# Scale factors of the first four heads from a quarter of the key and query weights, and the tail's squares in slots 10 to 15

## What is computed

```python
x = x + attn_a(layernorm(x))     # q = xn @ Wq[h] + bq, k = xn @ Wk[h] + bk, v = xn @ Wv[h] + bv
                                 # softmax(causal(q @ k.T / 8)) @ v per head, then @ Wo + bo
x = x + ffn(layernorm(x))        # relu(xn @ w1 + b1) @ w2 + b2
x = x + attn_b(layernorm(x))
x = x + ffn(layernorm(x))
```

## Time and profile before

| | us |
|---|---|
| median of 3 runs | 563.05 (561.37 to 563.49) |
| the profiled execution, first to last instruction | 561.3 |
| prologue, to the first instruction of slot 0 | 35.3 |
| one slot in the middle | 11.7 |

### The profile page before, as it was taken

How to read it: one execution, slowest core, us unless ns; L and a number is a source line. 1 busy time by engine, 2 the same in 40 slices (tenths; PEclk the granted TensorE clock), 3 DMA queues, 4 the chain that set the end, 5 groups by cost and what they waited for, 6 DMA issues and landing times.

```text
span 561.3 us, 17932 instructions
## 1 busy us (share of the span) xinstructions
PE 526.3 (94%) x6864; PEld 371.1 (66%) x6864; DVE 446.3 (80%) x1382; ACT 469.0 (84%) x925; POOL 453.8 (81%) x447
## 2 busy tenths in 40 slices
PE   4888999999999999999999999998989998798897
PEld 3654666666666666766667666675679695656576
DVE  5878888888888888888888888887785575788943
ACT  3888998999988999989999899998973978573995
POOL 5678989888888888888888888888983977654885
PEclk9979999999999999999999999999999999998999
DMA  9442343332433324333243332435147100000002
GB/s 227 109 113 57 72 110 86 96 96 68 114 87 97 95 64 118 87 95 96 60 122 80 102 97 58 124 78 198 40 151 272 68 3 2 1 1 2 1 21 57
DMA packets 35461, 48.03 MB, mean 86 GB/s; under 512 B 10777, under 2 KB 16817, under 8 KB 35377
## 3 DMA queue, kind: packets, MB, share of 16 engines
q1 hardware_dynamic: 33264, 46.35, 30.2%
q10 hardware_dynamic: 2112, 0.54, 0.4%
HBM read 12.27 MB, written 9.44 MB: 39 GB/s over the span
## 4 chain that ended last, share of the span: by engine, by line
PE 75%; DVE 8%; issue 6%; ACT 5%; POOL 5%; DMA 1%; DVEq 0%; POOLq 0%; ACTq 0%
PE psum L562 11%; PE psum L620 10%; PE psum L621 10%; PE psum L516 7%; PE psum L518 6%; PE psum L517 6%; PE psum L600 6%; PE psum L602 6%; PE psum L601 6%; PE psum L623 2%; POOL h_lo L2146 1%; PE psum L781 1%; POOL rstd L2024 1%; ACT xn L1164 1%; DVE st_lo L1515 1%
## 5 line engine op out<-in xcount | busy, mean ns | idle before, releaser
L2079 POOL TENSOR_TENSOR p_hl<-p,p_hl 128x512 f16<-128x512 f32 x288 | 328.5, 1165 | 48.4 <-ACT p_hl L1264 44.6
L1532 DVE CUSTOM_DVE_ANT_0 max_junk<-psum,mask_s 128x1024 bf16<-128x1024 f32 (+7 forms) x256 | 190.4, 753 | 32.7 <-issue 32.6
L1263 ACT ACTIVATE p<-psum 128x512 f32<-128x512 f32 x288 | 175.9, 611 | 13.8 <-PE psum L623 12.2
L1264 ACT ACTIVATE p_hl<-psum 128x512 f16<-128x512 f32 x288 | 177.2, 615 | 0.0
L620 PE MATMUL psum<-q_hl,k_hh 128*128 128x512 f16 (+3 forms) x384 | 125.6, 327 | 0.5 <-ACT p_hl L1264 0.4
L600 PE MATMUL psum<-v_all,p_hl 128*128 128x65 f16 x1152 | 124.8, 193 | 1.1 <-POOL p_hl L2079 1.0
L601 PE MATMUL psum<-v_all,p_hl 128*128 128x64 f16 x1152 | 124.9, 192 | 0.0
L602 PE MATMUL psum<-v_all,p_hl 128*128 128x65 f16 x1152 | 124.4, 194 | 0.0
L621 PE MATMUL psum<-q_hm,k_l 128*128 128x512 f16 (+3 forms) x384 | 122.3, 327 | 0.0
L600 PEld LDWEIGHTS psum<-v_all,p_hl 128*128 128x128 f16 x1152 | 107.1, 98 | 16.1 <-POOL p_hl L2079 1.2
L601 PEld LDWEIGHTS psum<-v_all,p_hl 128*128 128x128 f16 x1152 | 106.2, 97 | 4.8
(11 more groups left out here) (206 smaller groups left out, 1109.1 us busy)
## 6 DMA issues: line engine op xcount, KB each, us to landing
k_hh<-st_hi SPq DMA_DIRECT2D x64, 128.0 KB, 2.3
o_scratch<-o_sb SPq DMA_DIRECT2D x16, 512.0 KB, 2.6
o_in<-o_scratch SPq DMA_DIRECT2D x8, 1024.0 KB, 8.6
q_hl<-st_hi SPq DMA_DIRECT2D x32, 128.0 KB, 2.4
q_hl<-st_lo SPq DMA_DIRECT2D x32, 128.0 KB, 2.4
k_l<-st_lo SPq DMA_DIRECT2D x32, 128.0 KB, 2.3
q_hm<-st_hi SPq DMA_DIRECT2D x32, 128.0 KB, 2.4
x_sb<-in_L_attn_a_x SPq DMA_DIRECT2D x4, 256.0 KB, 3.9
```

The lines of the kernel that those rows point to most:

```text
L1263: nc.scalar.activation(p32[:, ring_at(u, r), :], src, ACT.Exp, scale=SCALE_A).then_inc(exp_done, 1)
L1264: nc.scalar.activation(p_hl[:, u % 2, 0, BANK * r:BANK * (r + 1)], src, ACT.Exp, scale=SCALE_A).then_inc(phi_done, 1)
L1532: nc.vector.tensor_tensor_reduce(out=max_junk[:, n % 2, 0:cols], in0=max_banks(v, j, 0, cols), in1=mask_s[:, S - cols:S], scale=1.0, scala ...
L2079: nc.gpsimd.tensor_tensor(p_hl[:, u % 2, 1, cols], p32[:, ring_at(u, r), :], p_hl[:, u % 2, 0, cols], ALU.subtract)\
```

## The change

- **Loads.** Wk and Wq are each loaded in two DMAs: heads 0 to 3 (a quarter) first, then the rest. The load of Wo comes after x chunks 2 and 3. The small loads (`bo`, `W_qk`, `W_v`, slope, `b1`, `b2`) are issued after the copies of the first pair.
- **Gains.** Heads 0 to 3 get key and query gains of their own from the first quarter and its biases. The other twelve heads get theirs later, in the middle of the maximum tiles of head 0 (`norm_kq(1)`, `gain_kq(1)`, `scale_bias(1)`). The roots are taken by integer steps on VectorE: the difference of two bit patterns, a quarter of it, the exponent bits. The powers on GpSimd and their operands `fourths` are gone.
- **Orders.** The pieces go in the order 0, 2, 1, 3. The square of Wv comes after their eviction. ScalarE now makes the scaled high half and the scaled copy of the rest of Wv. `first_stats(2)` stands before the low half of Wv, the first two maximum tiles stand between the value units, and the two `rest_scale` that are left stand between later maximum tiles. The counts and places of `idle_products` differ.
- **GpSimd and VectorE.** The memset of `k_l1` moves to the start of GpSimd's list and that of `q_hm` to the start of VectorE's. The memset of the rows of `k_l1` (8 partitions x 2048) now follows the second `chunk_rstd` and three selects.
- **Tail.** The six squares stand in slots 10 to 15, one each, ahead of that slot's last exponentials. Their sum, the transpose, `tail_norm` and `tail_gain` stand in slot 16, without GpSimd's power, and `tail_scales` in slots 17 to 19.

The core of the diff (declarations left out):

```diff
             load_x(0)
             load_x(1)
-            sp.dma_start(w_raw[:, 0, :].rearrange(...), Wk.rearrange("h e d -> e h d")).then_inc(wk_in, 16)
-            sp.dma_start(w_raw[:, 2, :].rearrange(...), Wv.rearrange("h e d -> e h d")).then_inc(wv_in, 16)
-            sp.dma_start(wo_raw[:, :, :], Wo.rearrange("(k p) e -> p k e", p=P)).then_inc(wo_in, 16)
-            sp.dma_start(bo_sb[:, :], bo.unsqueeze(1)).then_inc(bo_in, 16)
+            load_heads(0, Wk, 0, GH, wk_in[0])
+            load_heads(0, Wk, GH, H, wk_in[1])
+            load_heads(2, Wv, 0, H, wv_in)
             load_x(2)
             load_x(3)
+            sp.dma_start(wo_raw[:, :, :], Wo.rearrange("(k p) e -> p k e", p=P)).then_inc(wo_in, 16)
...
+            idle_products(14, 5)
+            pe.wait_ge(ones_ready, 1)
+            norm_sums(0, MAXB + 1)
             turn_chunk(0)
-            idle_products(8, 5)
+            idle_products(10, 5)
             turn_chunk(1)
-            idle_products(8, 5)
-            pe.wait_ge(sq_done, 4)
-            pe.wait_ge(ones_ready, 1)
-            nc.tensor.matmul(bank(MAXB + 1)[:, 0:4], ones[:, :], sums[:, 0:4], start=True, stop=True).then_inc(fro_full, 1)
-            idle_products(32, 5)
-            pe.wait_ge(first_lo, 2)
-            pe.wait_ge(xt_lo_done, 2)
-            for n in range(2):
+            idle_products(4, 5)
+            for n in FIRST_ORDER:
+                pe.wait_ge(first_lo, n // 2 + 1)
+                pe.wait_ge(xt_lo_done, n % 2 + 1)
                 piece(n, FIRST_BANKS[n])
...
+            values(0, V_BANKS[0])
+            max_tile(0, 0)
+            values(1, V_BANKS[1])
+            max_tile(0, 1)
+            values(2, V_BANKS[2])
+            values(3, V_BANKS[3])
+            norm_sums(1, V_BANKS[0])
+            max_tile(0, 2)
+            piece(4, V_BANKS[1])
+            max_tile(0, 3)
+            piece(5, V_BANKS[2])
+            max_tile(0, 4)
+            idle_products(8, 4)
...
+                nc.vector.tensor_tensor(apart, norms[:, k].bitcast(I32), norms[:, q].bitcast(I32), ALU.subtract).then_inc(root_done, 1)
+                nc.vector.tensor_scalar(quarter, apart, 0.25, QUARTER_ONE, ALU.mult, ALU.add).then_inc(root_done, 1)
+                nc.vector.tensor_scalar(gains[:, q].bitcast(I32), quarter, POW2, None, ALU.bitwise_and).then_inc(gain_made, 1)
...
             chunk_norm(0)
+            norm_kq(0, MAXB + 1)
+            gain_kq(0)
             chunk_norm(1)
-            norm_kq()
             chunk_low(0)
-            gain_kq()
-            chunk_low(1)
...
             norm_v()
             gain_v()
+            first_stats(2)
             first_low(2)
+            first_stats(3)
             dve.wait_ge(tri_ready, 2)
+            take_max(0, 0)
+            take_max(0, 1)
+            norm_kq(1, V_BANKS[0])
+            gain_kq(1)
+            scale_bias(1)
+            rest_scale(0)
+            take_max(0, 2)
+            rest_scale(1)
+            take_max(0, 3)
...
                 exponentials(u, 7)
+                if u in SQUARE_AT:
+                    tail_square(SQUARE_AT[u])
                 exponentials(u, 8)
```

More of the change, by code:

```diff
@@ L624, in scores, with idle_products @@
                 last.then_inc(st_full, 1)
+            def idle_products(n, dst):
+                for _ in range(n):
+                    nc.tensor.matmul(bank(dst)[:, 0:P], ident_b[:, :], ident_b[:, :], start=True, stop=True)
             def pe_slot(u):
@@ L701, in pe_slot @@
                     turn_chunk(3)
+                if u == SUMS_AT:
+                    pe.wait_ge(v_lo_done, units_after(u))
+                    pe.wait_ge(tail_sq, 6)
+                    nc.tensor.matmul(bank(MISC)[:, 3 * P:3 * P + 6], ones[:, :], tail_sums[:, :], start=True, stop=True).then_inc(prep_full, 1)
+                    nc.tensor.transpose(bank(MISC)[:, P:2 * P], wv2_raw[:, :], ident[:, :]).then_inc(prep_full, 1)
                 scores(u, 7)
@@ L707, in pe_slot @@
                 scores(u, 8)
-            def idle_products(n, dst):
-                for _ in range(n):
-                    nc.tensor.matmul(bank(dst)[:, 0:P], ident_b[:, :], ident_b[:, :], start=True, stop=True)
             pe.wait_ge(bias_in, 48)
@@ L732, in _ @@
-            for n in range(2, 4):
-                piece(n, FIRST_BANKS[n])
-            idle_products(12, 5)
+            idle_products(4, 5)
+            for n in FIRST_ORDER:
+                pe.wait_ge(first_lo, n // 2 + 1)
+                pe.wait_ge(xt_lo_done, n % 2 + 1)
+                piece(n, FIRST_BANKS[n])
+            idle_products(24, 5)
+            pe.wait_ge(sqv_done, 1)
+            nc.tensor.matmul(bank(MAXB + 1)[:, 4:5], ones[:, :], sums[:, 8:9], start=True, stop=True).then_inc(frov_full, 1)
@@ L1249, in _ @@
             act.wait_ge(v_lo_done, FIRST_UNITS)
-            for n in range(4, 6):
-                tail_square(n)
+            act.wait_ge(kq_ready, 4)
             def exponentials(u, r):
@@ L1616, in dve_slot @@
                 project(0)
-                tail_weights(0)
                 maximum(1)
@@ L1673, in norm_v, with scale_bias @@
+            def scale_bias(g):
+                cols = (slice(0, GH // 2), slice(GH // 2, OB))[g]
+                dve.wait_ge(inv_done, g + 1)
+                for which in range(2):
+                    nc.vector.tensor_scalar(b_kq[:, which, cols], b_cols[:, which, cols], gains[:, 2 * g + which:2 * g + which + 1], None, ALU.mult)\
+                        .then_inc(kq_ready, 1)
             def norm_v():
-                dve.wait_ge(fro_full, 2)
-                nc.vector.tensor_scalar(norms[:, 2:3], bank(MAXB + 1)[:, 4:5], float(E) * TOP_SQ, TINY_SQ, ALU.mult, ALU.add)\
-                    .then_inc(norm_done, 1)
+                dve.wait_ge(frov_full, 1)
+                nc.vector.tensor_scalar(norms[:, 4:5], bank(MAXB + 1)[:, 4:5], 2.0 * float(E) * TOP_SQ, 2.0 * TINY_SQ, ALU.mult, ALU.add)\
+                    .then_inc(normv_done, 1)
@@ L1696, in first_low @@
                 dve.wait_ge(first_hi, which + 1)
-                nc.vector.scalar_tensor_tensor(out=low, in0=src, scalar=gains[:, which:which + 1], in1=dst, op0=ALU.mult, op1=ALU.subtract)\
+                nc.vector.scalar_tensor_tensor(out=low, in0=src, scalar=gains[:, (0, 1, 4)[which]:(1, 2, 5)[which]], in1=dst, op0=ALU.mult, op1=ALU.subtract)\
                     .then_inc(first_lo, 1)
```

290 lines of the change are left out of this document (150 added, 140 removed).

## The result

| | before | after |
|---|---|---|
| median of 6 runs each, us | 562.21 (561.08 to 563.49) | 565.63 (565.42 to 567.3) |
| the profiled execution | 561.3 | 563.7 |

The ratio is 1.0066, with a 95% interval from 1.0046 to 1.0086. The changed kernel is slower by 3.4 us, and 561.7 had been predicted. The six runs of before lie in two groups, 561.1 to 561.4 and 563.1 to 563.5, and its median falls between them; the paragraph on the last part comes back to that. One run of 1371.91 us of a later experiment (`before_fill`) is left out everywhere.

The account below looks back on a forecast made before the run. TensorE was taken to bound middle slots (11.7 us each), with the start of slot 0 setting the rest. Prologue +0.9, slot 0 -2.8 and slots 10 to 16 +0.6 gave -1.3: 563.05 to 561.7 us, range 558.8 to 564.9.

Parts of the forecast that it names:

- gains at 9.4: Prologue: gains of the first heads done at 9.4 instead of 14.7, 5.3 us earlier.
- the memset of the rows holds the second chunk: Prologue: GpSimd's memset, 8.7 to 10.5, holds VectorE's first operation on chunk 1; chunk ready at 11.2, without hold 10.3.
- gain of Wv: Prologue: its square now follows the pieces; gain ready at 20.4, against 20.56 before, so the remaining 1.9 is gone.
- The squares: Slots 10 to 15: squares of Wo on ScalarE delay exponentials; 0.2 shows in slot 10, nothing in 11 to 15.
- The hold by the value subtractions: Prologue: GpSimd's four value subtractions, 25.5 to 29.9, hold VectorE's scaling and biases; between 0 and 2.2, taken as 0.5.
- rival C: Prologue: subtractions hold VectorE for two full units (2.2), TensorE idles, its clock falls; 566.4 us, chance 0.10.
- The clock ahead of slot 0: Before and into slot 0: TensorE's clock stays up thanks to small products, where before it was granted at 0.50.
- Prologue: Everything ahead of slot 0: +0.9 us, from -2.5 to +2.9.
- the clock in slot 0: Slot 0: with the clock up, VectorE's idle ahead of two maxima mostly goes; -2.2 us, 0 if it falls.
- the 0.6 for the tail operations: Slot 0: VectorE loses three tail operations between two maxima, about 0.2 each, saving 0.6 us.
- Slot 16 and 17: Slot 16: sum and transpose of the tail cost TensorE 0.4 us, where it is the bound.
- the late rise: Pieces in the prologue: TensorE's clock rises at 18 or so instead of 16.3, costing another 0.8 us.

Follow-up runs that it names:

- before_fill: The kernel before with 26 more small products in TensorE's gaps, behind maximum tiles 4 to 6; 561.7 us, ratio 0.9981.
- pool_order: The changed kernel with GpSimd's late 1/sqrt and shifts first and its value subtractions waiting for VectorE's scalings; 561.35 us, ratio 0.9986.
- order_gain: The changed kernel with GpSimd's order as in `pool_order` and tail_gain moved to slot 17 behind the first maximum; 561.9 us, ratio 0.9993.
- tail_only: The kernel before with the tail part of the change alone; 563.16 us, ratio 1.0033.
- mend_rows: `mend_dense` with the rows memset behind VectorE's low half of the second chunk and 12 instead of 20 products ahead of the second turn_chunk; 558.79 us, ratio 0.9955.
- fill_gap: The changed kernel with 48 instead of 8 small products behind maximum tile 4; 566.49 us, ratio 1.0082.
- rows_wait: The changed kernel with GpSimd's memset of the rows of k_l1 waiting for the second x chunk's normalization; 566.11 us, ratio 1.0059.
- gain_moved: The changed kernel with tail_gain moved from slot 16 to slot 17, behind the first maximum; 566.23 us, ratio 1.0077.
- fill_head: The changed kernel with 20 and 20 instead of 14 and 10 small products ahead of the pieces; 566.72 us, ratio 1.0088.
- mend_dense: `mend_head` with 24 more small products in the two gaps around maximum tile 4; 558.18 us, ratio 0.9932.
- mend_head: `order_gain` with 20 and 20 instead of 14 and 10 small products ahead of the pieces; 559.63 us, ratio 0.9945.

## Why the prediction was wrong

**Right**, step by step: gains at 9.4 (measured 9.06), the quarter landed at 6.3 (6.0), the memset of the rows holds the second chunk (1.40 for its first operation), the pieces at 12.5 and 0.43 apart (12.53, and so up to 15.1), last high half at 18.1 (17.3), gain of Wv used at 20.4 (19.6), first value copy at 24.4 (23.5). The squares: 0.2 was expected, 0 came.

**Wrong**:

- **The hold by the value subtractions**, the failed step. I knew the mechanism and both ends, 0 and 2.2, and took 0.5. It was 2.07. The reason I gave for the low value and against rival C was that the first of three scalings had begun inside a memset and all three took only 1.96. The memset was nearly over by then. The row of that one line in the kernel before, which I hadn't read, has the first scaling at 0.911 and the others at 0.60:

```profile
L1689 DVE TENSOR_SCALAR w_raw<-w_raw,gains x3: 602/609/911, 21.6 to 22.9; 128x768 f32<-128x768 f32 x3
```

 So that row had shown a hold of 0.3 by the rest of a memset, not that there is none. And I asked only after the scalings. The two bias operations, which I had at 0.4, took 1.50 for the same reason.
- **The clock ahead of slot 0.** I took it to stay up, for the small products. It stood at 0.50 from 32.2 to 39.0, after TensorE had idled 3.08. That cost 1.6 to 2.1 in the prologue on top of the holds and 0.7 in slot 0 (13.67 against 12.97 in `pool_order`), more than the holds did; slot 0 gained 1.37 instead of 2.8. Prologue: +0.9 predicted, +3.27 measured. With neither of these two holds nor a fall (`pool_order`) it is -0.43, so my sum of the other terms, +0.4, was 0.8 too high. That the holds bring the fall fits `pool_order`, which had neither, but `order_gain` fell at 33.4 without these holds, so they are not the only way to it. The 2.2 for the clock in slot 0 was the right size (2.20 in `before_fill`); the 0.6 for the tail operations is not shown. `tail_only` has 0.67 with the clock down, but part of that can be the earlier fall, and `pool_order`, with the clock up and those operations gone, takes no less than `before_fill` with them (12.97 and 12.84). I had added the two terms.
- **Slot 16 and 17.** +0.4 predicted, +2.00 measured: 0.63 for sum and transpose on TensorE, of which I had 0.4, and 1.12 for a hold of `tail_gain` plus 0.23 for the work itself. I had asked what GpSimd does beside the scalings in the prologue, but not beside three small operations in a slot in which GpSimd is busy for 10.2 of 11.7 us (20.33 in two slots).
- **The range.** It reached 3.2 above the forecast. My bounds of the prologue alone were +2.0 above its term, and by its own terms (2.2 for the hold, 0.8 for the late rise) the upper end was +3.4 and not the +2.9 that I wrote; the clock in slot 0 was worth another 2.2. The range was narrower than its terms.

What came is the mechanism of rival C: units paid in full, TensorE idle for three us, clock down. Its point of decision, a scaling that shows over 1.5, was met with 1.55. It had 0.10. That its time came close too, 566.4 against a measured 565.63, is in part luck: it charged 0.8 for a rise of the clock at 18, which came at 15.1, and nothing for the fall ahead of slot 0 (1.6 to 2.1) nor for the hold in slot 16 (1.12). With the row above read, the units should have been priced in full, and C with them.

## What to carry to other kernels

When an operation of VectorE moves, look up what GpSimd runs at its new time, also for the smallest operations: a hold lasts until GpSimd's instruction is over, whatever the size of the one that waits. Take the minimum, median and maximum of a line before a total of several is used as evidence against a hold. A stall of TensorE is paid twice where it pulls the clock down, so give the stall a second term; and compare fixed events slot by slot, or runs of the same mean granted clock, since ends of spans and medians hide 1 us here and 2 us there in stretches at the lower level.

## What the runs showed of the hardware

- GpSimd's memset and subtractions held VectorE's operations that read and write SBUF alone, on 128x128, 128x768, 128x6 and 128x5 numbers (1.40, 1.55, 1.50 for two, 1.15). Beside them operations that read PSUM kept their length (the low halves of pieces 0.68 each beside a memset in `mend_rows`), and so did the low halves of weights, with two inputs, beside a memset (0.87 for two). In the same stretch as the held biases, integer operations with one input on 128x1 took 0.15. The one with two inputs on 128x1 (`roots<-norms`, line 1720) took 0.16 in the changed kernel, where a subtraction was just over, but 0.45 in `fill_gap` and 0.77 in `rows_wait`, both times to the end of the subtraction beside it, so one column is no protection. The Trainium skill (SBUF — State Buffer, "SBUF: two separate sides") says that the lock lasts for the whole instruction of whoever came first, and that an operation of VectorE with two inputs in SBUF contends only with a GpSimd operation that reads there. The 1.15 beside GpSimd's 1.16, the 0.77 beside a subtraction, which reads, and the 0.87 beside a memset, which reads nothing, agree with it.
- Two executions of the same code up to 33 us, with gaps on TensorE of 0.25, 0.63 and 0.54 in one and 0.98 and 0.54 in the other, had different clocks there (`pool_order` 1.00, `order_gain` 0.50 for 3.4 us). A gain of 1 to 2 us in the slots, as in `gain_moved` and `before_fill`, hardly showed in a median.
- With 14 and 10 small products ahead of the pieces, five executions went to the higher level from the 7th to the 12th of the twelve matmuls (7th in the changed kernel, 12th in `pool_order`); the last one began between 16.16 and 17.05. With 20 and 20 it was the first in `fill_head` and `mend_dense`, but the third in `mend_head`. With 20 and 12, or with 14 and 10 but without the wait of 1.16 for the second chunk (`rows_wait`), it was the third. The rise came earlier where there were more products or a shorter wait, but between executions of the same code it alone moves the end of the pieces by up to 0.9 us.
- What made the clock stay up behind the gap of 3.07 in the run with 48 products and fall at 32.2 behind the 3.08 of the changed kernel was not settled. No run placed the same products at several distances from the gap.
